# Last block of a fused attention and feed-forward kernel: groups normalised before the last one, its sums packed for the reciprocal, modulation in a copy, output gate in the weights

## The reference

```
mod = (silu(c) @ wmod).reshape(6, 128)       # sa, ca, ga, sb, cb, gb
ga, gb: sign kept, magnitude at least 0.25
h = layernorm(x) * (1 + ca) + sa
x = x + ga * attention(h)                    # see below
h = layernorm(x) * (1 + cb) + sb
x = x + gb * ffn(h)

attention: v = log map of h; q, k, values = v @ Wq.T, v @ Wk.T, v @ Wv.T
           scores = (q * metric(h)) k / sqrt(8); a = softmax(scores)
           o = (a @ values) @ Wo.T
           out = project(mu + 0.1 * o)       # clip columns 1.. to -8..8,
                                             # column 0 = sqrt(1 + sum of squares + 1e-6)
ffn:       (silu(h @ wg.T) * (h @ wu.T)) @ wd.T, hidden width 384, weights int / 127
```

## Time and profile before

| | us |
|---|---|
| median of 3 runs (lowest, highest) | 607.02 (606.62, 607.74) |
| the profiled execution | 608.64 |
| its span in the trace | 606.6 |
| PE busy in it | 544.9 |
| ACT busy in it | 524.8 |
| DVE busy in it | 152.6 |
| mean granted PE clock | 0.951 of full |

### The profile page before, as it was taken

How to read it: one execution, slowest core, us unless ns; L and a number is a source line. 1 busy time by engine, 2 the same in 40 slices (tenths; PEclk the granted TensorE clock), 3 DMA queues, 4 the chain that set the end, 5 groups by cost and what they waited for, 6 DMA issues and landing times.

```text
span 606.6 us, 16308 instructions
## 1 busy us (share of the span) xinstructions
PE 544.9 (90%) x7196; PEld 239.8 (40%) x7196; DVE 152.6 (25%) x420; ACT 524.8 (87%) x595; POOL 21.5 (4%) x25
## 2 busy tenths in 40 slices
PE   1466998999979999999999999999999999999544
PEld 0232543554423334455323444554334444543122
DVE  6963303030310361100003611000016211000363
ACT  3564898999999999999999999999999999999401
POOL 2300100000000010000000100000001000000010
PEclk9576999999989999999999999999999999999958
DMA  6012267010030200001002100000000000010000
GB/s 186 3 37 84 91 164 183 3 35 3 28 106 1 70 22 10 3 11 37 10 3 53 37 11 1 11 27 20 2 10 2 11 1 11 2 45 1 1 0 23
DMA packets 13626, 20.64 MB, mean 34 GB/s; under 512 B 2027, under 2 KB 10347, under 8 KB 13267
## 3 DMA queue, kind: packets, MB, share of 16 engines
q1 hardware_dynamic: 12707, 17.22, 11.0%
q0 software_dynamic: 560, 1.97, 0.9%
q10 hardware_dynamic: 288, 0.40, 0.2%
HBM read 13.15 MB, written 4.19 MB: 29 GB/s over the span
## 4 chain that ended last, share of the span: by engine, by line
PE 64%; ACT 15%; DVE 7%; issue 7%; DMA 4%; SPq 1%; POOL 0%; ACTq 0%; DVEq 0%
PE ps L703 27%; PE ps L720 26%; ACT probs L510 13%; PE ps L639 8%; DMA K_op<-k_scr 2%; DVE probs L939 1%; DMA k_scr<-arena 1%; DMA probs<-x_dram 1%; PE ps L674 1%; PE ps L609 1%; DVE arena L1143 1%; ACT arena L440 1%; SPq L262 0%; DVE kmax L1008 0%; PE ps L735 0%
## 5 line engine op out<-in xcount | busy, mean ns | idle before, releaser
L510 ACT ACTIVATE probs<-ps 128x1024 f32<-128x1024 f32 x512 | 481.4, 1116 | 16.9 <-PE ps L703 15.3
L703 PE MATMUL ps<-Q_op,K_op 73*32 73x512 bf16 x4096 | 293.0, 381 | 10.7 <-ACT probs L510 6.7
L720 PE MATMUL ps<-probs,V_op 128*32 128x512 f32 x2048 | 273.1, 595 | 1.2 <-ACT probs L510 0.8
L703 PEld LDWEIGHTS ps<-Q_op,K_op 73*32 73x32 bf16 x4096 | 122.5, 96 | 232.7 <-issue 120.5
L720 PEld LDWEIGHTS ps<-probs,V_op 128*32 128x32 f32 x2048 | 71.3, 110 | 49.3 <-issue 5.4
L1100 DVE COPY O_sb<-ps 128x512 f32<-128x512 f32 x16 | 11.1, 692 | 154.4 <-PE ps L720 154.4
L560 PE MATMUL ps<-fixed_sb,arena 128*128 128x128 f32 x32 | 7.4, 391 | 15.1 <-POOL arena L384 11.1
L1203 DVE SCALAR_TENSOR_TENSOR arena<-arena,ps 128x512 f32<-128x512 f32 x12 | 8.3, 688 | 45.0 <-ACT arena L527 45.0
L522 ACT ACTIVATE arena<-ps 128x512 f32<-128x512 f32 x4 | 2.8, 705 | 18.5 <-PE ps L735 18.5
L1209 DVE TENSOR_TENSOR arena<-ps,arena 128x512 f32<-128x512 f32 x12 | 8.3, 692 | 40.4 <-PE ps L639 40.3
L378 POOL TENSOR_TENSOR small<-small,half 128x4 f32<-128x4 f32 x4 | 4.1, 1014 | 404.6 <-DVE small L1173 404.6
(11 more groups left out here) (162 smaller groups left out, 241.6 us busy)
## 6 DMA issues: line engine op xcount, KB each, us to landing
K_op<-k_scr SPq DMA_DIRECT2D x16, 288.0 KB
Q_op<-q_scr SPq DMA_DIRECT2D x9, 384.0 KB
arena<-O_sb SPq DMA_DIRECT2D x120, 16.0 KB
q_scr<-arena POOLq DMA_DIRECT2D x3, 384.0 KB, 3.0
probs<-x_dram SPq DMA_DIRECT2D x4, 256.0 KB, 5.2
x_res<-x_dram SPq DMA_DIRECT2D x4, 256.0 KB, 3.1
out_dram<-arena SPq DMA_DIRECT2D x4, 256.0 KB, 2.4
Q_op<-q_scr SPq DMA_DIRECT2D x3, 288.0 KB
```

The source lines that it names most:

```text
L510: act.activation(probs[:, 2 * ring(j) + half_, :], slot_bank(u % 3), ACT.Exp)\
L703: ins = pe.matmul(slot_bank(u % 3)[CW * c:CW * (c + 1), i, :], K_op[0:rows, kt // TPB, h, at_k:at_k + CW], Q_op[0:rows, at_q:at_q + BT], s ...
L720: ins = pe.matmul(O_bank[32 * i:32 * (i + 1), :], V_op[:, kt, VW * h:VW * h + 32], probs[:, 2 * ring(j) + i // 2, BT * (i % 2):BT * (i % 2 ...
```

## The change

1. `normalise` is called for rows 0 to 95 (the first three groups) before the last group's `evacuate`; rows 96 to 127 get their own path, `normalise_last`. For these PE first packs the denominators: 8 products of 64 columns against a 0/1 matrix put the one needed row per head and token on 32 rows by 64 columns (the denominators are 8-fold in the placed form). DVE takes maximum and reciprocal of the 32x64 tile, PE spreads the result back to 32x512 by 8 more products of 64 columns, and DVE multiplies. The placement of the numerators stands between packing and spreading, that of the denominators behind the spreading; `den_T` is now read by the checks alone.
2. The 0/1 matrices `spread` are a new input of 128x512 numbers (256 KB), loaded over `wmod_sb` by SP in the last block.
3. The factor 0.1 goes into the reciprocal, so the clip is one instruction. The gate product and the residual sum run ahead of the wait for the first root; column 0 of the residual is computed after it by one instruction on 4 columns.
4. The modulation by `cb` and `sb` leaves DVE (two instructions, L1195 and L1197) and becomes scale and bias of ACT's copy of the transposed tile. For it the two rows are turned into columns at the start of the kernel (2 products of one column, 1 copy). The first `keep_warm` has 5 products in place of 7.
5. `gb` is multiplied into the down weights once, in block 0, so the result is one sum from PSUM.

The diff, cut to its core:

```diff
+        spread_sb = wmod_sb[:, 0:2 * DH * GH * DH].rearrange("p (a b) -> p a b", a=2 * DH)
@@ SP, blocks
+                        if Bk == NB - 1 and g == 1:
+                            sp.wait_ge(S["Q_loaded"], 16 * QUERY_LOADS * Bk)
+                            sp.dma_start(wmod_sb[:, 0:2 * DH * GH * DH], spread).then_inc(S["spread_in"], 16)
@@ ACT
             k_split1(0)
+            act.wait_ge(S["cols_ps"], 1)
+            act.activation(mod_cols[:, :], M_bank[:, 0:2], ACT.Identity).then_inc(S["cols_sb"], 1)
@@
-                act.activation(h2_T, M_bank, ACT.Identity).then_inc(S["h2T_done"], 1)
+                act.activation(h2_T, M_bank, ACT.Identity, scale=mod_cols[:, 0:1],
+                               bias=mod_cols[:, 1:2]).then_inc(S["h2T_done"], 1)
@@ PE, last tail
                 pe.wait_ge(S["o_evac"], NG * (last + 1))
+                few = BT // DH
+                pe.wait_ge(S["spread_in"], 16)
+                for c in range(DH):
+                    ins = pe.matmul(bank(2)[96:128, 0:few], spread_sb[:, c, :], O_sb[:, NG - 1, few * c:few * (c + 1)],
+                                    start=c == 0, stop=c == DH - 1, tile_position=(0, 96))
+                ins.then_inc(S["den_packed"], 1)
                 pe.matmul(bank(0)[96:128, :], place_num, O_sb[:, NG - 1, :], start=True, stop=True,
-                          tile_position=(0, 96))
+                          tile_position=(0, 96)).then_inc(S["num_placed"], 1)
+                pe.wait_ge(S["rec_packed"], p + 1)
+                for c in range(DH):
+                    ins = pe.matmul(bank(3)[96:128, few * c:few * (c + 1)], spread_sb[96:128, DH + c, :],
+                                    rec_few[96:128, :], start=True, stop=True, tile_position=(96, 96))
+                ins.then_inc(S["rec_spread"], 1)
                 pe.matmul(bank(1)[96:128, :], place_den, O_sb[:, NG - 1, :], start=True, stop=True,
-                          tile_position=(0, 96)).then_inc(S["placed"], 1)
+                          tile_position=(0, 96)).then_inc(S["den_placed"], 1)
                 t_wo(last)
                 pe.wait_ge(S["epow_out"], 2 * (last + 1))
-                keep_warm(7, bank(5))
+                keep_warm(5, bank(5))
@@ DVE, block 0
+            dve.tensor_tensor(wd_f[:, :, :], wd_f[:, :, :], row3(5, NM), ALU.mult).then_inc(S["ffn_ready"], 1)
@@ DVE, Tail
+                    c.did(dve.tensor_scalar(rec_T[rows, :], den_T[rows, :], SUM_FLOOR, 10.0, ALU.max, ALU.mult))
+                def normalise_last(self):
+                    c, rows = self.c, slice(96, P)
+                    dve.wait_ge(S["den_packed"], self.p + 1)
+                    c.did(dve.tensor_scalar(rec_few[rows, :], bank(2)[rows, 0:BT // DH], SUM_FLOOR, 10.0,
+                                            ALU.max, ALU.mult))
                     c.after()
+                    dve.reciprocal(rec_few[rows, :], rec_few[rows, :]).then_inc(S["rec_packed"], 1)
+                    dve.wait_ge(S["num_in"], self.p + 1)
+                    dve.wait_ge(S["rec_spread"], self.p + 1)
+                    dve.tensor_tensor(att_T[rows, :], num_T[rows, :], bank(3)[rows, :], ALU.mult)\
+                        .then_inc(S["norm"], 1)
+                    dve.wait_ge(S["den_in"], self.p + 1)
@@ residual
-                    c.did(dve.tensor_scalar(flat, M_bank, 0.1, 8.0, ALU.mult, ALU.min))
-                    c.after()
-                    c.did(dve.tensor_scalar(flat, flat, -8.0, None, ALU.max))
+                    c.did(dve.tensor_scalar(flat, M_bank, 8.0, -8.0, ALU.min, ALU.max))
@@
-                    c.did(dve.tensor_tensor(h2, h2, row3(4, TPB), ALU.mult))
-                    c.after()
-                    dve.tensor_tensor(h2, h2, row3(3, TPB), ALU.add).then_inc(S["h2_done"], 1)
@@ result, last block
-                            c.did(dve.tensor_tensor(y[:, t, :], bank(DOWN_BANK[t])[:, P * t:P * (t + 1)],
-                                                    mod[:, 5 * D:6 * D], ALU.mult))
+                            ins = dve.tensor_tensor(y[:, t, :], bank(DOWN_BANK[t])[:, P * t:P * (t + 1)], x1[:, t, :],
+                                                    ALU.add)
-                    dve.tensor_tensor(y, y, x1, ALU.add).then_inc(S["y_ready"], 1)
```

More of the change, by code:

```diff
@@ L76, in after, with build @@
         self.eng.wait_ge(self.sem, self.start + self.n)
-def build(nc, x, columns, wmod, fixed, w1t, w2t, w_att, wgt, wut, wdt, out):
+def build(nc, x, columns, wmod, fixed, w1t, w2t, w_att, wgt, wut, wdt, spread, out):
     with ExitStack() as ctx:
@@ L593, in _ @@
                 metric1(0, m)
+            pe.wait_ge(S["mod_full"], 1)
+            for i, m in enumerate((4, 3)):
+                ins = pe.matmul(M_bank[:, i:i + 1], mod[0:1, D * m:D * (m + 1)], flag_f[0:1, 1:2], start=True, stop=True)
+            ins.then_inc(S["cols_ps"], 1)
             def v_T(b):
@@ L625, in q_of @@
                 if b == 0:
+                    pe.wait_ge(S["cols_sb"], 1)
                     ins = pe.matmul(M_bank, wq_sb, vT[:, b, :], start=True, stop=True)
@@ L1127, in __init__, with normalise @@
                     self.c = Chain(dve, S["tail"], Bk * TAIL_STEPS + MORE * p)
-                def normalise(self, placed=False):
+                def normalise(self, rows=slice(0, P)):
                     Bk, c = self.Bk, self.c
@@ L1133, in normalise @@
                         dve.wait_ge(o_in[g], 16 * 2 * GH * (Bk + 1))
[L1134 to L1138, removed]
-                    else:
-                        dve.wait_ge(o_in[NG - 1], 16 * 2 * GH * (Bk + 1 - self.p))
-                        c.did(dve.tensor_scalar(rec_T, den_T, SUM_FLOOR, None, ALU.max))
-                    c.after()
-                    c.did(dve.reciprocal(rec_T, rec_T))
-                    c.after()
-                    if placed:
-                        dve.wait_ge(S["num_in"], self.p + 1)
-                    dve.tensor_tensor(att_T, num_T, rec_T, ALU.mult).then_inc(S["norm"], 1)
+                    if rows.stop == P:
+                        dve.wait_ge(o_in[NG - 1], 16 * 2 * GH * (Bk + 1 - self.p))
+                    c.did(dve.tensor_scalar(rec_T[rows, :], den_T[rows, :], SUM_FLOOR, 10.0, ALU.max, ALU.mult))
+                    c.after()
+                    c.did(dve.reciprocal(rec_T[rows, :], rec_T[rows, :]))
+                    c.after()
+                    ins = dve.tensor_tensor(att_T[rows, :], num_T[rows, :], rec_T[rows, :], ALU.mult)
+                    if rows.stop == P:
+                        ins.then_inc(S["norm"], 1)
+                    else:
+                        c.did(ins)
+                def normalise_last(self):
[3 more added lines that the diff above has]
+                                            ALU.max, ALU.mult))
+                    c.after()
+                    dve.reciprocal(rec_few[rows, :], rec_few[rows, :]).then_inc(S["rec_packed"], 1)
[4 more added lines that the diff above has]
+                    dve.wait_ge(S["den_in"], self.p + 1)
                 def checks(self):
@@ L1180, in residual @@
                     c.did(dve.tensor_tensor(x1, x1, x_res[:, :, :], ALU.add))
+                    c.after()
+                    dve.wait_ge(S["epow_out"], 2 * Bk + 1)
+                    c.did(dve.scalar_tensor_tensor(x1[:, :, 0], x0, mod[:, 2 * D:2 * D + 1], x_res[:, :, 0],
+                                                   ALU.mult, ALU.add))
                     c.after()
@@ L1247, in blocks @@
                 last = NB * (p + 1) - 1
+                tail = Tail(last, NB - 1, p)
+                tail.normalise(slice(0, 96))
                 evacuate(last, NG - 1)
-                tail = Tail(last, NB - 1, p)
-                tail.normalise(placed=True)
+                tail.normalise_last()
                 tail.residual()
@@ L1286, in _ @@
                 blocks(1)
-_NAMES = ["x", "columns", "wmod", "fixed", "w1t", "w2t", "w_att", "wgt", "wut", "wdt"]
+_NAMES = ["x", "columns", "wmod", "fixed", "w1t", "w2t", "w_att", "wgt", "wut", "wdt", "spread"]
 def kernel(**inputs):
@@ L1301 @@
     mu[0] = 1.0
+    spread = np.zeros((P, 2, DH, GH, DH), np.float32)
+    for j in range(GH):
+        for c in range(DH):
+            spread[32 * j + DH + c, 0, c, j, c] = 1.0
+            spread[96 + DH * j + c, 1, c, j, :] = 1.0
+    spread = spread.reshape(P, 2 * DH * GH * DH)
     heads = np.repeat(np.eye(H, dtype=np.float32), DH, axis=0)[by_dim]
@@ L1315 @@
         "wgt": a["L0_ffn_w_gate"].T, "wut": a["L0_ffn_w_up"].T,
+        "spread": spread,
         "wdt": a["L0_ffn_w_down"].T.reshape(NM, P, D).transpose(1, 0, 2).reshape(P, NM * D),
```

39 lines of the change are left out of this document (23 added, 16 removed).

## The result

| | before | after |
|---|---|---|
| median us (runs) | 607.04 (6) | 599.43 (6) |
| lowest, highest | 604.70, 608.01 | 598.33, 601.03 |
| profiled execution | 608.64 | 601.03 |
| its span | 606.6 | 599.2 |

The ratio after/before is 0.9866, 95% interval 0.9845 to 0.9887: 1.34% faster. Between the medians lie 7.6 us (1.25%). The forecast was 599.8.

The account below looks back on a forecast made before the run. From the last evacuation to the store, 32.15 us, each instruction waits for the one before. Savings and losses, 4.68 + 1.57 + 0.81 - 0.41 + 0.71 - 0.14 = 7.22 us, off the 607.02 median give 599.8; range 598.6 to 602.0.

Parts of the forecast that it names:

- the four parts: Last evacuation to store, split at projection's end, layer norm and feed-forward's start: 4.68, 1.57, 0.81 and 0.71 us saved.
- the stretch: From the last evacuation's end at 568.42 to the store at 600.57: 32.15 us of instructions waiting one for another.
- Part A: Last evacuation to projection's end: early groups covered, fourth group packed, projection at full clock; 4.98 us for 9.66, 4.68 saved.
- The rival that weight loads set their pace: Narrow products of packing and spreading: 0.11 us each, not 0.055, adding 1.8 us, total 601.6; chance 0.14.
- Part B: Projection's end to layer norm: clip and column copy removed, product and sum beside the root; 3.55 us for 5.12, 1.57 saved.
- room of 0.37: Residual before the layer norm: the root was to end 0.37 us before the sum and so be hidden.
- the rival took one that excludes the other: Residual: root and the two wide DVE instructions cannot overlap; 4.65 us there, 1.1 lost, total 600.9; chance 0.10.
- The row at 16.31: Profile row read as two DVE products beside a POOL instruction, 1.41 us in all, 0.70 each, nothing lost.
- Part C: Layer norm to feed-forward: 5 warming products for 7, gates 4.06 us after the second root for 4.87; 0.81 saved.
- The clock: Start of feed-forward: PE's clock rises 5.26 us after the first warming product, 1.20 us at half clock; 0.41 lost.
- The bounds I gave: Feed-forward's clock loss: from nothing lost (rise before 4.06 us) to 0.8 us lost (rise one us later).
- The stream: ACT's three copies before the last tail: two column operands cost 0 to 0.09 us more each; 0.14 lost.

Follow-up runs that it names:

- e4: Kernel before, plus 16 unread warming products behind the placements, ahead of the projection; ratio to before 0.9990.
- e2: Kernel after, but gate product and residual sum wait for the first root again; one run, 599.65 us.
- e5: Kernel after with 7 warming products after the second root in place of 5; ratio to before 0.9894.
- after_again: Kernel after, unchanged, measured once more beside new runs of the kernel before; ratio to before 0.9891, median 599.54 us.
- e9: e7 with a plain ACT copy and DVE's modulations in blocks 0 to 2; ratio to before 0.9858, median 597.86 us.
- e7: Kernel after with unread products on PE all the way from the projection to the transposes; ratio to before 0.9873.
- e1: Kernel after with only early groups and packed sums; residual, modulation, 7 warming products and output gate as before the change; ratio to before 0.9934.
- e3: Kernel after without packing and spreading: the fourth group's maximum and reciprocal run on 512 columns; ratio to before 0.9945.
- e6: Kernel after with 2 warming products after the second root in place of 5; ratio to before 0.9894.

## Why the prediction was right, point by point

**The place.** All of the gain lies between the last evacuation and the store, and each of the four parts was worth what its links said, within 0.2: 7.61 for 7.36 in the stretch.

**Part A**, 4.50 for 4.68. The steps held: cover for the early groups (DVE's idle time before the last evacuation shrank from 28.14 to 16.80, never to nothing), reciprocal by width (0.56 for 0.55), maximum 0.24 for 0.25, narrow products at the column pace. 16 of them took 1.09 and 1.07 from start to last result, for 1.05 forecast and 0.11 more for a load ahead of the second 16. The rival that weight loads set their pace would have shown 1.9. So the Trainium skill's rule (TensorE: Matmul & The Clock Gate, part on packing small matmuls, The mechanism) that loads overlap running products only where the row group differs is not what these rows show: all 16 products of the packing use the same rows and columns of the array, and their 16 loads, 0.92 us busy, lie inside PE's 1.08. Projection at full clock: 1.01 for 1.05, and shown by e4 to be clock. What was a little off, 0.2 in all, is the placement ahead of the projection (0.98 on the chain for 0.86) and the way from its end to the clip (0.10 for 0.02).

**Part B**, 1.40 for 1.57. I had the two instructions beside the root cost nothing, and left room of 0.37. The root grew by 0.37, which used up the room, and the sum on 4 columns waited 0.25 for it: 0.17 in all. Of the two sides that the Trainium skill's sentence on shared interfaces (GPSIMD Engine Reference, Key points) leaves open, the rival took one that excludes the other (1.1 lost). e2 shows a third: POOL is slowed, DVE is not, and only in part. One premise of the forecast was misread. The row at 16.31 is one DVE instruction of 1.41, not two of 0.70; the other instructions of that line and shape take 0.68 to 0.69. So beside POOL it took 0.7 longer, as the one at 18.09 did (1.23 for 0.28), and no row had shown a wide DVE instruction free of cost there. That the two moved ones were free was right, but by luck. A difference in the rows is that at 16.31 and 18.09 POOL had started first, while at the root DVE had (575.61, POOL 575.78). It does not explain all of it, for the sum at 576.32 began inside the root and took its plain 0.69. No run tests the order.

**Part C**, 0.83 for 0.81. e5 confirms the mechanism: with 7 products the gates are 0.85 later. ACT's copy takes 0.79, not 0.69: the forecast took the row of one column operand for two, and each adds 0.09 to the plain 0.60. PE's two unread products (0.85) ended no earlier, so the slip cost nothing.

**The clock** was the term of the sum with the wrong sign: forecast 0.41 lost, measured 0.14 gained. I took the rise 5.26 us after the first warming product, as in the one execution I had. It was 3.83 in the profiled execution after, 4.5 in `after_again`, and between 3.07 and 5.20 in the six other kernels whose clock fell. So it differs between executions; for a median a value between would have been the better estimate, with little or nothing lost. The bounds I gave did not hold it. They stopped at "nothing lost" for a rise before 4.06, but the feed-forward before has itself 0.39 us at half clock, so such a rise gains up to 0.2, and 0.14 is what came.

**The stream** was the term mis-sized the other way: 0.14 forecast, 0.50 measured. The step took the row of one column operand, 0.69 against 0.60, for an upper bound, and halved it. Two operands cost 0.17, and ACT passes on all of it. The terms were off by 0.55 for the clock, and by 0.36 for the stream, 0.18 for A and 0.17 for B the other way. They nearly cancel: stream and last tail together gave 7.11 for the 7.22 forecast. That 599.8 came so near is therefore in part luck. The stretch ahead of the stream, where nothing was forecast, adds 0.27.

**Elsewhere.** The load costs nothing: e9 has it and the stream of the kernel before. The new products and the copy at the start and the longer weight preparation lie ahead of the stream, where the traces differ by up to 3.25 us. None shows a cost there, and none could show a small one: the stream starts at 195.00 to 197.98 in the nine with the new products, at 197.88 and 198.25 in the two without.

The medians agree better than single runs can: before the stream's start (the evacuation at 198.25) the traces differ by these 3.25 us, 195.00 in e7 and 198.25 before. PE's granted clock goes with it: between 30 and 60 us it is 0.69 before and after, 0.77 in `after_again` (stream from 195.58) and 0.78 in e7. What makes it differ was not tested.

## What to carry to other kernels

In a tail where one engine works at a time, sum the links: each removed instruction is worth its whole duration plus its hand-over (the 0.02 to 0.07 us to the next start), and the sum came out within 0.3 of 7.4 us, two of its errors cancelling. Read the count at the end of a row before its duration is used: one long instruction and two short ones lead to opposite conclusions. An elementwise instruction's time here follows its columns (reciprocal: 0.25 us at 16, 0.55 at 64, 3.35 at 512, on 32 rows as on 128), so a repeated row is worth packing before a slow operation, even at the price of two sets of small products, and the more so if they keep PE from going idle. An operand added to an instruction of the engine that is always late costs in every repetition; put it only where the chain is serial.

## What the runs showed of the hardware

- PE's clock rose 3.07 (e4), 3.77 (e1), 3.83 (after), 3.97 (e2), 4.43 (e5), 4.5 (`after_again`), 4.93 (e3), 5.20 (e6) and 5.26 us (before) after the first of the products that follow the second root, in nine executions. A tail that starts its warming late draws a lot each time, worth up to a us here. Unread products with gaps of 0.22 to 0.66 us between them kept the clock at 1.00 (e7), and the links of DVE and POOL kept their lengths.
- DVE instructions of 128x512 with two SBUF inputs beside a POOL root on 4 columns: POOL 1.38 for 1.01, DVE unchanged (0.68, 0.69). Beside a POOL product of 128x512 that had started first, such a DVE instruction took 1.41 for 0.69.
- A copy of 128x512 by ACT: 0.60 plain, 0.78 with two column operands in the tail; 0.74 and 0.91 in the stream.
- 16 float32 product instructions of 64 columns in one column group: 1.08 us, 0.06 each.
